# One block for attention and experts: first expert's weights and six batches' tokens prepared during the attention's drain

## The reference

```python
x = _layernorm(x + _L0_attn_ref(x, ...))            # state space + MLP
x = _layernorm(x + _L0_xattn_ref(x, ctx_2048, ...)) # 16 query heads, 4 key/value heads, head size 128
x = _layernorm(x + _L0_ffn_ref(x, ...))
```

```python
scores = einsum('blhd,bmhd->bhlm', q, k_full) * scale + mask   # context keys and causal own keys
out = einsum('bhlm,bmhd->blhd', softmax(scores), v_full)
return out.reshape(B, L, 2048) @ wo
```

```python
logits = einsum('th,eh->te', xt, w_router)
topk_w, topk_i = top_k(sigmoid(logits), 2);  topk_w /= sum(topk_w)
expert_out = einsum('tei,ehi->teh', silu(xt @ wg) * (xt @ wu), wd)
out = einsum('te,teh->th', comb, expert_out) + both shared experts
```

## Time and profile before

| | |
|---|---|
| median of three runs | 779.17 us (778.35 to 784.29) |
| the profiled execution | 787.61 us, of which the span from first to last instruction is 785.9 us |
| mean granted TensorE clock | 0.973 of 2.4 GHz |
| attention's loop and drain | up to 486.2 us in the span |
| experts | from 489.0 us |
| busy: TensorE, VectorE, ScalarE, GpSimd | 722.3, 564.8, 472.9, 344.0 us |

### The profile page before, as it was taken

The page is one execution under the profiler, slowest core; times in us unless marked ns, Lnnn a source line. Parts: engine busy times, 40 slices in busy tenths (PEclk is TensorE's granted clock), DMA queues, the critical chain, the costliest instruction groups (busy, mean ns, idle before and its releaser), DMA issues. The chain is left out here.

```text
span 785.9 us, 15318 instructions
## 1 busy us (share of the span) xinstructions
PE 722.3 (92%) x5030; PEld 657.3 (84%) x5030; DVE 564.8 (72%) x1176; ACT 472.9 (60%) x1066; POOL 344.0 (44%) x512
## 2 busy tenths in 40 slices
PE   4998888788999999999999987998999999999965
PEld 3887677577889999999899976986999999999855
DVE  4864588876878888887878773664587778776436
ACT  4454666456877777777777772342577777776301
POOL 0002566596988787877787751063000000000341
PEclk9999999998999999999999999699999999999978
DMA  9003300100200000000600000266356766670121
GB/s 290 4 1 115 134 2 0 30 5 28 62 8 1 7 0 7 0 7 0 207 0 0 0 1 9 96 240 209 115 161 227 250 203 210 227 241 28 54 67 54
DMA packets 45940, 64.82 MB, mean 82 GB/s; under 512 B 4288, under 2 KB 34880, under 8 KB 45632
## 3 DMA queue, kind: packets, MB, share of 16 engines
q1 hardware_dynamic: 39936, 56.39, 21.7%
q0 software_dynamic: 1536, 4.20, 1.6%
q10 hardware_dynamic: 4416, 3.58, 1.6%
HBM read 53.14 MB, written 11.01 MB: 82 GB/s over the span
## 5 line engine op out<-in xcount | busy, mean ns | idle before, releaser
L1816 POOL DMA_INDIRECT gu_raw<-rows_out,slot x16 | 15.5, 972 | 203.6 <-DMA rows_out<-y_sb 199.0
L1951 ACT ACTIVATE sg<-bg 128x256 f32<-128x256 f32 (+1 forms) x95 | 40.7, 429 | 104.1 <-PE bg L68 101.6
L413 ACT ACTIVATE under_dt<-two,nb,under_raw 128x256 f32<-128x256 f32 x128 | 70.6, 561 | 45.5 <-DVE nb L496 45.5
L66 PE MATMUL bg<-xb_hi,gu_hi 128*128 128x256 f32 x300 | 87.0, 290 | 2.7 <-DVE xb_lo L2064 2.7
L2041 DVE TENSOR_TENSOR hf<-sg,bg 128x256 f32<-128x256 f32 (+1 forms) x95 | 45.1, 475 | 58.1 <-ACT sg L1951 56.6
L68 PE MATMUL bg<-xb_hi,gu_lo 128*128 128x256 f32 x300 | 85.6, 285 | 0.0
L67 PE MATMUL bg<-xb_lo,gu_hi 128*128 128x256 f32 x300 | 85.5, 285 | 0.0
L66 PE MATMUL two<-under_h 128*128 128x256 f32 (+1 forms) x208 | 66.9, 322 | 2.9 <-PEq L117 1.5
L68 PE MATMUL bd<-dn_hi,eh_lo 128*128 128x256 f32 x220 | 63.1, 287 | 3.9 <-issue 3.8
L67 PE MATMUL bd<-dn_lo,eh_hi 128*128 128x256 f32 x220 | 62.9, 286 | 3.0 <-issue 3.0
L594 POOL TENSOR_SCALAR under_dt<-under_dt,rec 128x256 f32<-128x256 f32 x128 | 61.5, 499 | 6.4 <-DVE rec L542 6.4
(11 more groups left out here) (294 smaller groups left out, 2555.6 us busy)
## 6 DMA issues: line engine op xcount, KB each, us to landing
gu_raw<-in_gu SPq DMA_DIRECT2D x17, 1280.0 KB
dn_raw<-in_dn SPq DMA_DIRECT2D x17, 640.0 KB
rows_in<-under_dt SPq DMA_DIRECT2D x1, 3840.0 KB, 13.1
rows_out<-y_sb SPq DMA_DIRECT2D x30, 128.0 KB, 2.1
x_blk<-rows_in ACTq DMA_DIRECT2D x13, 256.0 KB, 2.7
under_raw<-in_wq SPq DMA_DIRECT2D x1, 2048.0 KB, 8.1
under_raw<-in_wkv SPq DMA_DIRECT2D x1, 2048.0 KB, 12.7
under_raw<-in_wo SPq DMA_DIRECT2D x4, 512.0 KB, 3.9
```

Of the source, the lines that this page charges most:

```text
L66: pe.matmul(out, lh, rh, start=first, stop=False)
L413: act.activation(self.prob[:, g % 2, h, :], self.b_s[:, h // 2, (h % 2) * MW:(h % 2 + 1) * MW], ACT.Exp, bias=self.nb[:, h:h + 1], scale=s ...
L1816: pool.indirect_dma_start(got[k][:, b, :], None, ys[:, :], bass.IndirectOffsetOnAxis(ap=slot[:, k, b:b + 1], axis=0)).then_inc(f_got[b], 16)
L1951: act.activation(sg[:, u % 3, 0:width(u)], gate_of(u), ACT.Silu).then_inc(f_sg, 1)
```

## The change

Attention and experts become one block; all semaphores are taken once and cleared at the end. `experts` is called first and returns functions; each engine's attention program is followed by its expert program, and some pieces are called inside the drain. In SBUF, the first weights and the three x buffers (`gu_raw0, dn_raw0, gu_hi0, gu_lo0, x_hi, x_lo, x_f`) now lie on the right side over the attention's projection weights; in PSUM the banks are those of the attention.

```diff
 pe_tail:
         self.pe_turn_p(pe, 2, N2, None)
+        for q in range(3):
+            self.ex.pe_turn_x(pe, self, q)
         self.pe_out(pe, LAST, 1, N1)
         self.pe_values(pe, 2, N2)
         self.pe_turn_p(pe, 3, N3, None)
+        self.ex.pe_logits(pe, 0)
         self.pe_out(pe, LAST, 2, N2)
         self.pe_values(pe, 3, N3)
+        self.ex.pe_logits(pe, 1)
         self.pe_out(pe, LAST, 3, N3)
 act_tail:
         self.act_p(act, N1)
+        self.ex.act_weights(act, 0)
+        self.ex.act_weights(act, 1)
         self.act_exp(act, 3, N3)
         self.act_o(act, N1)
         self.act_p(act, N2)
+        for q in range(3):
+            self.ex.act_x(act, q)
         self.act_o(act, N2)
 dve_tails:
         self.dve_p(dve, N2)
+        self.ex.dve_x(dve, 0)
+        self.ex.dve_x(dve, 1)
         self.dve_o(dve, N2)
         self.dve_p(dve, N3)
+        self.ex.dve_x(dve, 2)
         self.dve_o(dve, N3)
 pool_tail:
             self.pool_step(pool, LAST, g, False, True)
+            if g >= 2:
+                self.ex.pool_weights(pool, g - 2)
 sp_program (attention), at its end:
+        sp.wait_ge(self.a_pj, NS)
+        self.ex.load_first(sp)
 pe_program (attention), at its end:
-        self.pe_spare(pe, self.b_q[:, 0:DM], 28)
 experts, new:
+        turned = (bd[0], bd[1], bg[0], bx[1])
+        def pe_turn_x(pe, at, q):
+            pe.wait_ge(at.a_x2, 2 * q + 2)
+            if q == 0:
+                pe.wait_ge(at.a_exp, NS * AREP)
+            elif q == 2:
+                pe.wait_ge(at.a_qlo, NS)
...
+        def pe_logits(pe, b):
...
+            pe.wait_ge(r_f, b // 2 + 1)
...
+        def act_weights(act, s):
+            if s == 0:
+                act.wait_ge(e_gu[0], 16)
+            act.activation(gu_hi[0][:, s, :, :], gu_raw[0][:, s, :, :], ACT.Copy).then_inc(w_gh[0], 1)
+        def pool_weights(pool, s):
+            pool.wait_ge(w_gh[0], s + 1)
+            pool.tensor_tensor(gu_lo[0][:, s, :, :], gu_raw[0][:, s, :, :], gu_hi[0][:, s, :, :].bitcast(F32),
+                               ALU.subtract).then_inc(w_gl[0], 1)
 experts, TensorE, ahead of the rounds:
-                for q in range(4):
...
-                spare(pe, bx[1][:, 0:256], x_hi[:, 0, 0:P], x_hi[:, 0, 0:256], 16)
+            for b in range(2, 5):
+                pe_logits(pe, b)
+            pe_turn_x(pe, at, 3)
+            for b in range(5, BATCH):
+                pe_logits(pe, b)
 experts, TensorE, round 0:
-                    if q == 0:
-                        spare(pe, bd[1][:, 0:256], x_hi[:, 0, 0:P], x_hi[:, 0, 0:256], 28)
 experts, ScalarE, ahead of the rounds:
-                act.dma_start(upper[:, :], a["upper"]).then_inc(r_c2, 16)
...
-                round_gu(0, 0)
-                round_gu(0, 1)
+            act_x(act, 3)
 experts, SP, ahead of load(1):
-                load(0)
+            sp.wait_ge(at.a_x2, BATCH)
+            sp.wait_ge(s_zero, 16)
+            sp.dma_start(upper[:, :], a["upper"]).then_inc(r_c2, 16)
 experts, GpSimd, first:
+            pool.wait_ge(at.a_x2, BATCH)
 experts, VectorE, ahead of the logits: the four splits of x and both rests of weights 0 are gone
+            dve.wait_ge(s_zero, 16)
 experts, VectorE, round 0, in order:
 before: gated(0), gated(1), rest_h(0), rest_h(1), places, owners, rest_dn(0), shares, gated(2), gated(3), rest_h(2), gated(4), rest_h(3)
 after:  gated(0), dve_x(3), gated(1), places, gated(2), rest_h(0), rest_h(1), owners, gated(3), rest_h(2), gated(4), rest_h(3), rest_dn(0), shares
```

More of the change, by code:

```diff
@@ L7 @@
+from collections import namedtuple
 from contextlib import ExitStack
@@ L132, in decoder_layer @@
         ys = nc.dram_tensor("rows_out", (NBLK * BLK, DM), F32, kind="Internal").ap()
+        ex = experts(nc, a, scope, sem, ident, x_tok, acc, wr, rank, s_router, xs, ys, s_zero, out)
         with ExitStack() as both:
[L135 to L137 removed]
+            at = Attention(scope(both)[0:2] + (sem,), nc, a, ident, x_tok, s_zero, xs, ex)
+            state_space_layer(nc, a, scope, sem, ident, x_tok, acc, s_const, at, wr, rank, s_router)
 class Region:
@@ L739, in state_space_layer @@
         upper, lower = aw.upper, aw.lower
[L740 to L741 removed]
+        s_wout = kept("s_wout")
+        s_norm_w = kept("s_norm_w")
         with ExitStack() as part:
@@ L1645, in outputs_before, with experts @@
     return sum(4 if shared(g) else 2 for g in range(q))
-def experts(nc, a, scope, ident, x_tok, accm, wr, rank, s_router, xs, ys, s_zero, out):
+Programs = namedtuple("Programs", ("load_first", "pe_turn_x", "pe_logits", "act_x", "act_weights", "pool_weights", "dve_x", "sp_program", "pool_program",
+                                   "pe_program", "act_program", "dve_program"))
+def experts(nc, a, scope, sem, ident, x_tok, accm, wr, rank, s_router, xs, ys, s_zero, out):
     NG_ = NBLK + 4
@@ new lines, in experts @@
+        turned = (bd[0], bd[1], bg[0], bx[1])
[5 more added lines that the diff above has]
+                pe.wait_ge(at.a_qlo, NS)
+            for k in range(KT):
+                for b in range(2):
+                    mm = pe.transpose(turned[q][:, k * 256 + b * P:k * 256 + (b + 1) * P],
+                                      x_tok[:, 2 * q + b, k * P:(k + 1) * P], ident[:, :])
+            mm.then_inc(r_t, 1)
@@ new lines, in pe_logits, with act_x @@
+        def pe_logits(pe, b):
+            if b == 0:
+                pe.wait_ge(s_router, 32)
+            pe.wait_ge(r_f, b // 2 + 1)
+            for k in range(KT):
+                mm = pe.matmul(bd[0][:, b * E:(b + 1) * E], x_f[:, k, b * P:(b + 1) * P], wr[:, k, :],
+                               start=(k == 0), stop=(k == KT - 1))
+            if b == BATCH - 1:
+                mm.then_inc(r_l, 1)
+        def act_x(act, q):
+            act.wait_ge(r_t, q + 1)
+            act.activation(x_f[:, :, q * 256:(q + 1) * 256], turned[q][:, :].rearrange("p (k t) -> p k t", k=KT),
+                           ACT.Copy).then_inc(r_f, 1)
@@ new lines, in pool_program @@
+        def pool_program(pool, at):
+            pool.wait_ge(at.a_x2, BATCH)
+            pool.wait_ge(s_zero, 16)
+            pool.memset(mh[:, :], -0.5).then_inc(f_mh, 1)
+            pool.memset(ones[:, :], 1.0).then_inc(f_mh, 1)
+            pool.wait_ge(r_slot, 1)
+            for b in range(BATCH):
+                for k in range(2):
+                    pool.indirect_dma_start(xs[:, :], bass.IndirectOffsetOnAxis(ap=slot[:, k, b:b + 1], axis=0),
+                                            x_tok[:, b, :], None).then_inc(r_scat, 16)
+            for n in range(4):
+                pool.wait_ge(f_ys[n], 16 * ((2 * NBLK - n + 3) // 4))
+            pool.wait_ge(w_gl[0], 2 * (LASTW // 2 + 1))
+            pool.wait_ge(w_gl[1], 2 * (LASTW // 2))
+            for b in range(BATCH):
+                for k in range(2):
+                    pool.indirect_dma_start(got[k][:, b, :], None, ys[:, :],
+                                            bass.IndirectOffsetOnAxis(ap=slot[:, k, b:b + 1], axis=0)
+                                            ).then_inc(f_got[b], 16)
+            pool.wait_ge(f_mh, 1)
+            for n, (lo, hi) in enumerate(ROOTS):
+                pool.wait_ge(f_mv, hi)
+                pool.tensor_scalar(ve[:, lo:hi], mv[:, lo:hi, 1], 1.0, LN_EPS, ALU.mult, ALU.add).then_inc(f_ve, 1)
+                pool.wait_ge(f_ve, n + 1)
+                pool.tensor_tensor(rstd[:, lo:hi], ve[:, lo:hi], mh[:, lo:hi], ALU.pow).then_inc(f_r, 1)
```

913 lines of the change are left out of this document (437 added, 476 removed).

## The result

The median went from 784.14 us (20 runs, 778.35 to 786.56) to 773.88 us (20 runs, 771.82 to 780.68): a ratio of 0.9893, 95% interval 0.9872 to 0.9913. A later measurement gave 0.9916 (0.9886 to 0.9946; 775.95 against 782.51 us). The change makes the kernel about 1% faster. The forecast, 765.4 us with a range of 756 to 771, was too low. The profiled execution of the changed kernel took 773.47 us (span 771.8): 14.1 less than the profiled one of before, where 13.8 had been forecast. That these two sentences stand side by side is the lesson of the case. One thing is needed to read them: the 20 executions of the kernel before lie in two groups, six at 778 to 781 us and the others at 783 to 787; experiments 4 and 7 show why.

The account below looks back on a forecast made before the run. TensorE, busy 92% of the span, was taken as the bound, gains lying in its waits and half clock. Gains of 18.2 us less 2.0 and 2.6, plus 0.2, made 13.8; from 779.2, 765.4 us, range 756 to 771.

Parts of the forecast that it names:

- The step that failed: Closing arithmetic: the 13.8 us gain worked out on the 787.6 us profiled execution was subtracted from the 779.2 us median.
- Barrier and hand-over: Between attention and experts: removing the barrier gains 2.8 us; early weights, turning and logits gain 10.4 us.
- VectorE's order: Shared expert's first half: tile 2's product ahead of owners, down rests and shares removes TensorE's wait, gaining 4.1 us.
- Half clock on tiles 0 to 3: First four shared-expert tiles: time lost to half clock before the change is saved, 0.9 us.
- GpSimd beside VectorE: Attention's drain: GpSimd's subtractions for the first weights slow VectorE, costing 2.0 us, ends 0.3 and 3.5.
- Clock: Hand-over without spares: TensorE's clock falls, slowing matmuls from 490.4 and the last logits, costing 2.6 us.
- Rows for the blocks: Expert blocks: slots come 11.8 us earlier, plus 1.9 of slack makes 13.7, just enough not to delay TensorE.
- (A): Rival, chance 0.20: GpSimd's subtractions fall into VectorE's waits and the clock stays, so no cost bites; 761.1 us.
- (B): Rival, chance 0.11: shifted instruction stream removes TensorE's stall in output product 17, 9.5 us more gained; 756 us.
- (C): Rival, chance 0.11: roundings or splits hold the drain 3.5 us and late slots make expert blocks wait; 771.5 us.
- (D): Rival, chance 0.03: TensorE's starvation beside GpSimd's indirect DMAs grows, 20.5 us more lost; 786 us, slower.
- The marks: Signs named for the new profile, including first shared matmul at about 490.8; another length of output product 17 would disprove.

Follow-up runs that it names:

- run 4: Kernel before, profiled a second time without any edit; the profiled execution took 779.93 us, against 787.6 us in its first profile.
- 7: Kernel before without the 28 spare matmuls that end its attention block; median 787.43 us.
- run 2: Changed kernel with 12 + 4 spare matmuls put back on TensorE around the last batches' turning and logits; 773.32 us against 773.88.
- run 3: Changed kernel with VectorE's old order in the first half of the shared expert; 781.33 us against 773.88.
- run 1: Changed kernel with GpSimd's two subtractions for the first expert's weights moved to VectorE; 771.06 us against 773.88.
- runs 12: Changed kernel with the first weights' subtractions on VectorE and the gathers in two groups of eight, without spare matmuls; 764.03 us.
- 13: Changed kernel with the first weights' subtractions on VectorE, 12 + 4 spare matmuls and gathers in two groups, measured once more; 762.07 us.
- run 6: Changed kernel with only the eight gathers of the first choice, the second expert's part left out; 764.90 us against 773.88.
- runs 9: Changed kernel with the first weights' subtractions on VectorE, 12 + 4 spare matmuls and the sixteen gathers in two groups of eight; 763.09 us.
- 10: Changed kernel with weight subtractions on VectorE, 12 + 4 spares, gathers in two groups, and scatters in two groups, the second waiting for the first's landing; 765.11 us.
- 14: Changed kernel with weight subtractions on VectorE, 12 + 4 spares, gathers in two groups, and five tile fillings as a pause before the ninth scatter; 761.03 us.

## Why the prediction was wrong, by its own steps

**The step that failed** is the last: "The median of the runs shown is 779.2, 8.4 less; the same step from it gives 765.4." The step of 13.8 us was worked out on an execution whose hand-over ran at half clock from 490 to 503. Part of what the change was credited with, 12.6 us of hand-over and 0.9 of half clock in the tiles, was that execution's half clock. An execution of 779 us has part of this gain already: in run 4 the hand-over and the first tiles are 4.4 us shorter. From run 4 (779.93) to the profiled changed kernel (773.47) is 6.5 us, from the first profile 14.1; the 13.8 less these 4.4 and less the 1.9 that GpSimd cost beyond its term (below) would be 7.5. The prediction's own sum, 787.6 - 13.8 = 773.8, was the time of the changed kernel's 20 runs, in part by luck (below), and the further step was not due: what comes out behind the hand-over does not keep the 8.4 us that separated two executions of the old one. That profile and median lay 8.4 us apart was known; which stage held them was not asked. Nor is 13.8 the step between the two kernels: it is 10.3 us between the medians of 20 runs each (784.14 and 773.88) and 6.6 in the later measurement (782.51 and 775.95). The range's ends were moved down by the same 8.4; without that they are 764 and 779, and hold the result. What the chances said, faster by over 1%, came out at the edge: 1.1% and 0.8%.

**The terms, one by one**, in the frame of the drain's last reduction but one:
- *Barrier and hand-over*, 13.2 in the forecast: from x_tok to the first tile 15.4 us became 3.6, 11.8 gained; with the clock held (run 2) it is 2.3. Right, less the clock.
- *VectorE's order*, 4.1: the wait measured 3.97 (run 3) and brings 1.0 of lost clock with it, 5.0 at block 0.
- *Half clock on tiles 0 to 3*, 0.9: run 4 shows 0.9 on that stretch, but only because that execution had kept its clock longer.
- *GpSimd beside VectorE*, 2.0 with ends of 0.3 and 3.5: 3.9 in the profile, 3.8 undone by run 1. The term that was mis-sized most. The scaling was put at +0.7 from a neighbour that had 0.68 beside GpSimd and measured +1.7; the cast at +0.65 from its slowest value (931 against 278 ns) and measured +2.7. The slow values of the earlier trace rows were taken as the price; they are instructions that began when at most 0.8 us of a GpSimd instruction was left. The scaling and the cast began with 1.84 and 2.84 us left and were held for all of it, as the two ends above show.
- *Clock*, 2.6: at half speed from some 487.8 to some 494.6. The logits and transposes lost more (1.3 us up to the first tile, run 2 against the changed kernel), the tiles less (3.0 us at half speed, 1.5 lost). Together 2.8; 2.0 in the times (runs 12 and 13). Right.
- *Rows for the blocks*, "just enough": TensorE did not wait for block 0.
- *What the sum left out*: 2.1 us that the attention stage happened to lose in the profile of before. It was in no term and came out of the comparison as a gain. It made up for the contention's extra 1.9, which is why the sum met the profiled time to 0.3 us. That hit is in part luck.
- *Not in the forecast at all*: TensorE starved beside the scatters. The first output product took 9.95 us in one profile and 16.1 and 16.6 in two others, against 8.4 to 9.8 with the old order. It is one reason for the changed kernel's own spread up to 781.

**The rivals.** (A) is out: both costs bit. (B) is out: the stream is 144 instructions shorter and the first hole still lies 13 to 14 us behind the first gather, as in every profile with sixteen gathers in one go. Its 9.5 us were real, though, in the timed runs too (run 6: 9.0 less by the medians). (C) had the right price for the splits and the wrong rest: no block waited for rows. (D) named the mechanism of the scatters' 6 us, at a smaller size than it feared.

**The marks** set beforehand were met: no gap of 2.8 us, the load at 450, the roundings ahead of the softmax, tile 4 without a gap, the clock at 0.5 around 488 to 494. The last two subtractions of line 551 came 2.2 and 1.8 us later, as marked, but with the drain's lead of 2.1 counted they are some 4 late. The first shared matmul came at 491.58 where 490.8 was named, or 2.9 late once the drain's lead of 2.1 is counted; 1.9 of that is the contention, the rest the half clock ahead of it. One mark spoke against the sum, another length of output product 17: it took 12.07 us in place of 16.6. But the starving behind it goes on into the tiles, and from block 0 to the end the kernel is only 0.6 us shorter than before.

What stays open: what it is that TensorE lacks while GpSimd's indirect DMAs run. That they cause it (run 6) and that a pause ends it (runs 9, 10, 12, 13, 14) is shown. That it is the supply of instructions is not: no load of queue 8 stands in the starving beside the gathers. Also open is why one execution of the changed kernel loses 2.6 us and another 9 beside the same scatters; the half clock is part of the 9, but what sets it off so differently is not shown.

## What to carry to other kernels

A sum worked out on one execution gives the changed kernel's time from that execution; before it is moved to a median, find the stage that holds the difference, since a change that removes this stage removes the difference with it. A VectorE instruction with two operands in SBUF, or a cast between two tiles in SBUF, that begins inside a long GpSimd subtraction should be priced at the whole rest of that subtraction. Sixteen indirect DMAs in one go can starve TensorE 13 us later; a pause of 2.0 us in the middle of the gathers brought 4 to 9 us here, a new wait of 2.7 included, more than most edits.

## What the runs showed of the chip

- VectorE can be held for the rest of a GpSimd instruction, however small its own work: beside subtractions of 1,280 columns two columns took 1.85 us in place of 0.16, 512 columns 3.13 in place of 0.42, both ending within 0.3 us of GpSimd's. The Trainium skill, "SBUF — State Buffer", section "SBUF: two separate sides", has it that the port pair that the two engines share is "an exclusive lock, not a bandwidth split", held for the whole instruction; beside the subtractions the trace agrees with this and not with the fractions that the forecast took. It does not agree for every GpSimd instruction: beside the power of six columns, which reads SBUF too, the scaling was not held in any of 30 cases (0.16 us). Nor was the reduction that reads PSUM (0.69 us inside the subtraction).
- TensorE stalls in a chain without waits, 13 to 14 us behind the first of sixteen gathers in each of the ten profiles that have them in one go, and not at all in that product where eight run without more (7.36 us) or where they pause (7.35). The Trainium skill, "Runtime: NRT & Kernel Launch", section "Instruction fetch mechanics", calls the cost at the borders of instruction blocks mostly hidden. Whether the 9 us are such a cost is not shown; no load of TensorE's instructions falls into these stalls.
- The granted clock fell 4.0 us behind the last x_tok in one execution of the kernel before and 7.9 us behind it in another (run 4); the hand-over and the first tiles differed by 4.4 us for it, with nothing in the program different.
